# Router logits computed the other way round, and the work in front of the attention loop reordered

## What is computed

```
# block 1: attention, 16 heads of 64, one shared key/value head, a null key from cond_64
q = l2norm(ln(x) @ Wq) * q_scale;  k = l2norm(ln(x) @ Wk) * k_scale;  v = ln(x) @ Wv
x = x + ln(softmax(8 q k^T + relative bias + mask, null column) v @ Wout)
# block 2: mixture of 8 experts (the best 2) and a shared one of double width
logits = (x @ wt.T + cond_64 @ wg.T) / 2          # one of 8 per token
scores = softmax(logits); w = top 2 of scores, divided by their sum
y = sum_k w_k * (leaky(x @ w_gate[e_k]) * (x @ w_up[e_k])) @ w_down[e_k] + shared part
x = x + y
```

## Time and profile before

| | |
|---|---|
| median of 3 runs | 1135.11 us (1134.98 to 1137.51) |
| profiled execution | 1139.32 us, its span 1137.4 us |
| mean granted TensorE clock | 0.976 |
| busy, share of the span | TensorE 90%, VectorE 69%, ScalarE 46%, POOL 39% |
| chain that ended last | TensorE 66%, VectorE 20%, ScalarE 5%, issue 6% |

### The profile page before, as it was taken

How to read it: one execution, slowest core, us unless ns; L and a number is a source line. 1 busy time by engine, 2 the same in 40 slices (tenths; PEclk the granted TensorE clock), 3 DMA queues, 4 the chain that set the end, 5 groups by cost and what they waited for, 6 DMA issues and landing times.

```text
span 1137.4 us, 22612 instructions
## 1 busy us (share of the span) xinstructions
PE 1028.3 (90%) x7340; PEld 843.4 (74%) x7340; DVE 781.0 (69%) x2538; ACT 526.0 (46%) x1563; POOL 443.3 (39%) x422
## 2 busy tenths in 40 slices
PE   2377899999999999899999999899998999999898
PEld 1265587777877788677877787777877778777777
DVE  6768858775687648775587747876597756866442
ACT  2048724663356614655255623565146642566111
POOL 3154414553435505453336424354145433355112
PEclk9688999999999999999999999999999999999999
DMA  5064411321123212321123111221113211232033
GB/s 203 19 177 158 150 38 56 104 85 57 40 80 98 66 40 74 103 66 38 58 91 96 59 55 58 92 68 65 59 56 103 84 38 33 81 103 65 20 104 119
DMA packets 40939, 89.89 MB, mean 79 GB/s; under 512 B 4128, under 2 KB 18976, under 8 KB 40304
## 3 DMA queue, kind: packets, MB, share of 16 engines
q1 hardware_dynamic: 40816, 88.29, 24.3%
HBM read 78.67 MB, written 11.70 MB: 79 GB/s over the span
## 4 chain that ended last, share of the span: by engine, by line
PE 66%; DVE 20%; issue 6%; ACT 5%; POOL 1%; DMA 1%; SPq 1%; DVEq 0%; ACTq 0%; POOLq 0%
PE psY L1460 11%; PE psO L1393 6%; PE psS L1363 5%; PE psG L63 4%; PE psG L65 4%; PE psG L64 4%; PE psT L1374 3%; PE psS L63 3%; PE psS L64 3%; DVE work L1042 3%; PE psS L65 3%; PE psS L1358 2%; PE psO L1396 2%; PE psT L63 2%; PE psT L65 2%
## 5 line engine op out<-in xcount | busy, mean ns | idle before, releaser
L552 POOL TENSOR_TENSOR work<-work,rden 128x514 f32<-128x514 f32 x128 | 134.3, 1049 | 329.1 <-DVE rden L1023 328.5
L1460 PE MATMUL psY<-Wd,H 128*128 128x256 f32 x640 | 166.7, 395 | 3.7 <-POOL H L566 3.7
L675 ACT ACTIVATE work<-work,low 128x257 f32<-128x257 f32 x256 | 128.3, 503 | 80.7 <-DVE low L1042 80.6
L63 PE MATMUL psG<-x1T_hi,Wgu 128*128 128x512 f32 x280 | 128.1, 458 | 11.7 <-ACT leaky L707 9.8
L1460 PEld LDWEIGHTS psY<-Wd,H 128*128 128x128 f32 x640 | 113.3, 189 | 32.3 <-issue 15.6
L1042 DVE CUSTOM_DVE_ANT_0 work<-psS,bias,null_s 128x256 f32<-128x256 f32 x256 | 113.0, 478 | 18.3 <-PE psS L1363 18.0
L1132 DVE SCALAR_TENSOR_TENSOR leaky<-leaky 128x512 f32<-128x512 f32 x80 | 55.6, 695 | 101.5 <-ACT leaky L707 100.5
L541 POOL TENSOR_TENSOR rq<-qss,neghalf 128x16 f32<-128x16 f32 x32 | 93.7, 2930 | 55.0 <-DVE qss L1017 55.0
L65 PE MATMUL psG<-x1T_lo,Wgu 128*128 128x512 f32 x280 | 110.3, 394 | 0.0
L64 PE MATMUL psG<-x1T_hi,Wgu 128*128 128x512 f32 x280 | 109.6, 391 | 0.0
L667 ACT ACTIVATE qT_hi<-psO 128x256 fp32r<-128x256 f32 x128 | 48.9, 382 | 108.8 <-PE psO L1396 107.7
(11 more groups left out here) (242 smaller groups left out, 2677.4 us busy)
## 6 DMA issues: line engine op xcount, KB each, us to landing
Wgu<-wexp SPq DMA_DIRECT2D x80, 512.0 KB, 3.5
Wb<-wscr SPq DMA_DIRECT2D x64, 256.0 KB, 3.7
wexp<-Wgu SPq DMA_DIRECT2D x10, 512.0 KB, 2.9
xin<-in_x SPq DMA_DIRECT2D x8, 512.0 KB, 4.1
xres<-in_x SPq DMA_DIRECT2D x8, 512.0 KB, 5.0
out<-work SPq DMA_DIRECT2D x8, 512.0 KB, 3.1
H<-in_wgu SPq DMA_DIRECT2D x10, 256.0 KB, 3.8
bscr<-bscr SPq DMA_DIRECT2D x1, 2048.0 KB, 13.0
```

The source lines that it names most:

```text
L63: te.matmul(dst, a_hi, b_hi, start=start, stop=False)
L552: pool.tensor_tensor(T1[sl][:, hs, :], T1[sl][:, hs, :], rden[sl][:, 1, hs].unsqueeze(2) .to_broadcast([P, 2, N + 1]), ALU.mult)
L675: act.activation(T1[sl][:, h, :], T1[sl][:, h, :], ACT.Exp, scale=-1.0, bias=low[sl][:, 1, h:h + 1], accum_out=den[sl][:, 1, h:h + 1])
L1460: mm = te.matmul(psY[:, t // 2, (t % 2) * D:(t % 2 + 1) * D], H[:, k % H_RING, t * P:(t + 1) * P], Wd[:, ORDER[k], :], start=(k == 0 and t ...
```

## The change

The router's logits are computed with Wt as the stationary operand: WtP holds [Wt_hi, Wt_lo] (16 columns), so that two matmuls of 512 columns with x1T_hi and two with x1T_lo give 16 rows of psO, of which rows 0 to 7 and 8 to 15 have to be added. ScalarE copies them to LT; `turn_logits` multiplies LT by I2 (two identities of 8 on top of each other), which adds and transposes them into psY, from where `router_logits` reads. WT becomes the first 8 rows of LT.

ScalarE makes both halves of x1T_hi and all of KB_hi; VectorE makes KB_lo in one operation. `null_scores` uses tensor_reduce over an axis of length 1 instead of tensor_copy. The subtraction of the maximum becomes a function of its own behind `sum_q` 1. Gate 0 stands right behind the logits and no longer waits for the router; both query halves of tile 3 stand in front of gate 1, up 1 between the turned queries, gate 2 behind them. Three of the four half downs of blocks 0 and 1 move to loop steps 1 to 3. The orders of ScalarE and VectorE follow. Behind the last attention VectorE puts leak 0 and hidden 0 between the router's parts, and ScalarE the exponential and WT behind gates 0 and 1.

```diff
-DOWN_AT = {4: (2, FIRST), 5: (2, SECOND), ...
+DOWN_AT = {1: (0, SECOND), 2: (1, FIRST), 3: (1, SECOND), 4: (2, FIRST), 5: (2, SECOND), ...
@@ scalar: attention
-                    if t >= 2 and moe is not None:
-                        take_gate(moe, t - 2)
+                    if t == 2 and moe is not None:
+                        take_gate(moe, 0)
+                        softmax(moe)
...
                     if t == 1:
                         if moe is not None:
-                            softmax(moe)
+                            logits(moe)
                         need(act, kdT_ps, r, 1)
-                        act.activation(KB[0][0:DH, :, :], psO[0:DH, :]...
+                        act.activation(KB[0][:, :, :], psO[:, :]...
+                if moe is not None:
+                    take_gate(moe, 1)
                 for n in range(4):
                     turned_q(r, n)
-                    if n == 1 and moe is not None:
-                        take_gate(moe, 2)
+                if moe is not None:
+                    take_gate(moe, 2)
...
             def route(m):
-                need(act, x1T_ps, m, 1)
-                act.activation(x1T[0][:, 0, :], psG[:], ACT.Copy).then_inc(x1T_a.sem, 1)
+                for c, bank in ((0, psG), (1, psO)):
+                    need(act, x1T_ps, m, c + 1)
+                    act.activation(x1T[0][:, c, :], bank[:], ACT.Copy).then_inc(x1T_a.sem, 1)
+
+            def logits(m):
+                need(act, lt_ps, m, 1)
+                need(act, wscr_in, m - 1, 16)
+                act.activation(LT, psO[0:2 * E, :], ACT.Copy).then_inc(lt_done.sem, 1)
@@ vector: attention
                 sum_q(r, 1)
+                if moe is not None:
+                    router_shift(moe)
                 need(dve, kdT_ps, r, 1)
-                dve.tensor_copy(KB[0][DH:P, :, :], kT[DH:P]).then_inc(kb_v.sem, 1)
-                for i, ev in ((0, kb_a), (1, kb_v)):
...
+                need(dve, kb_a, r, 1)
+                dve.tensor_tensor(KB[1][:, :, :], psO[:, :]..., KB[0][:, :, :]..., ALU.subtract)
...
                 sum_q(r, 2)
                 if moe is not None:
                     router_best(moe)
+                scale_q(dve, r, 1, qn_done)
+                sum_q(r, 3)
+                if moe is not None:
                     leak(moe, 1)
-                scale_q(dve, r, 1, qn_done)
-                if moe is not None:
-                    hidden(moe, 1)
-                sum_q(r, 3)
                 for n in range(4):
                     turned_q(r, n)
                     if n == 1 and moe is not None:
-                        leak(moe, 2)
+                        hidden(moe, 1)
                         router_weights(moe)
+                scale_q(dve, r, 2, qn_done)
                 if moe is not None:
+                    leak(moe, 2)
                     hidden(moe, 2)
-                scale_q(dve, r, 2, qn_done)
                 scale_q(dve, r, 3, qn_done)
@@ tensor: attention
                     logits(moe)
+                    gate(moe, 0)
+                    turn_logits(moe)
                 need(te, kd_done, r, 1)
...
-                if moe is not None:
-                    gate(moe, 0)
                 q_half(2, 1).then_inc(q_ps.sem, 1)
                 if moe is not None:
                     up(moe, 0)
                 need(te, qs_done, r, 2)
                 q_half(3, 0)
+                q_half(3, 1).then_inc(q_ps.sem, 1)
...
                 if moe is not None:
                     gate(moe, 1)
-                q_half(3, 1).then_inc(q_ps.sem, 1)
-                if moe is not None:
-                    up(moe, 1)
                 for n in range(4):
                     turn_q(r, n)
                     if n == 1 and moe is not None:
-                        gate(moe, 2)
+                        up(moe, 1)
                 if moe is not None:
+                    gate(moe, 2)
+                    down(moe, 0, FIRST)
                     up(moe, 2)
-                    down(moe, 0, WHOLE)
-                    down(moe, 1, WHOLE)
...
             def logits(m):
+                need(te, x1T_v, m, KC)
+                for c in range(KC):
+                    te.matmul(psO[0:2 * E, :], WtP[:, c, :], x1T[0][:, c, :], start=(c == 0), stop=False, ...)
+                for c in range(KC):
+                    mm = te.matmul(psO[0:E, :], WtP[:, c, 0:E], x1T[1][:, c, :], start=False, stop=(c == KC - 1), ...)
+                mm.then_inc(lt_ps.sem, 1)
+
+            def turn_logits(m):
+                need(te, lt_done, m, 1)
+                need(te, ysum, m - 1, TILES)
                 for t in range(TILES):
+                    mm = te.matmul(psY[:, 0, t * E:(t + 1) * E], LT[:, t * P:(t + 1) * P], I2, start=(t == 0), stop=True, ...)
                 mm.then_inc(lg_ps.sem, 1)
```

More of the change, by code:

```diff
@@ L136, in attention_moe @@
         PARTS = ("hi", "lo")
-        Wall = [sb(f"Wall_{part}", [P, KC, E + KVN + HEADS * DH], F32R) for part in PARTS]
-        KV0, Q0 = E, E + KVN
+        Wall = [sb(f"Wall_{part}", [P, KC, KVN + HEADS * DH], F32R) for part in PARTS]
+        KV0, Q0 = 0, KVN
+        WtP = sb("WtP", [P, KC, 2 * E], F32R)
+        I2 = sb("I2", [2 * E, E])[:]
         Wout = [sb(f"Wout_{part}", [P, PAIRS, D], F32R) for part in PARTS]
@@ L715, in _ @@
             route(ROUNDS - 1)
-            softmax(ROUNDS - 1)
-            weights(ROUNDS - 1)
+            logits(ROUNDS - 1)
             for k in range(BLOCKS):
                 take_gate(ROUNDS - 1, k, True)
+                if k == 0:
+                    softmax(ROUNDS - 1)
+                if k == 1:
+                    weights(ROUNDS - 1)
         @block.vector
@@ L801, in kv_parts @@
             def kv_parts():
[L802 to L805, removed]
+                for src, hi, lo in ((Wkvn_in, *(part[:, :, KV0:Q0] for part in Wall)),
+                                    (Wt[:], WtP[:, :, 0:E], WtP[:, :, E:2 * E])):
+                    pre(dve.tensor_copy(hi, src))
+                    pre(dve.tensor_tensor(lo, src, hi.bitcast(F32), ALU.subtract))
             def others():
@@ L1030, in null_scores @@
                 for tile, T, n in ((1, T1, N), (0, T0, P)):
[L1031 to L1032 removed]
+                    dve.tensor_reduce(T[sl][:, :, n], null_s[:, 2 * bb + tile, h0:h0 + GH].unsqueeze(2), AX, ALU.add)
             def scores(r, g, s):
@@ L1119, in x1_parts @@
             def x1_parts(m):
[L1122 to L1125, removed]
+                for c, bank in ((0, psG), (1, psO)):
+                    need(dve, x1T_a, m, c + 1)
                     dve.tensor_tensor(x1T[1][:, c, :], bank[:], x1T[0][:, c, :].bitcast(F32),
@@ L1158, in _ @@
             router_logits(m)
+            router_shift(m)
+            leak(m, 0)
             router_best(m)
+            hidden(m, 0, True)
             router_weights(m)
-            for k in range(BLOCKS):
+            for k in range(1, BLOCKS):
                 leak(m, k)
@@ L1408, in logits @@
             def logits(m):
[L1409 removed]
+                need(te, x1T_v, m, KC)
+                for c in range(KC):
+                    te.matmul(psO[0:2 * E, :], WtP[:, c, :], x1T[0][:, c, :], start=(c == 0), stop=False, skip_group_check=True)
+                for c in range(KC):
+                    mm = te.matmul(psO[0:E, :], WtP[:, c, 0:E], x1T[1][:, c, :], start=False, stop=(c == KC - 1),
+                                   skip_group_check=True)
+                mm.then_inc(lt_ps.sem, 1)
+            def turn_logits(m):
+                need(te, lt_done, m, 1)
+                need(te, ysum, m - 1, TILES)
                 for t in range(TILES):
[L1411 to L1415 removed]
+                    mm = te.matmul(psY[:, 0, t * E:(t + 1) * E], LT[:, t * P:(t + 1) * P], I2, start=(t == 0), stop=True,
+                                   skip_group_check=True)
                 mm.then_inc(lg_ps.sem, 1)
@@ L1484, in _ @@
                 gate(m, k, True)
+                if k == 0:
+                    turn_logits(m)
                 up(m, k, True)
```

50 lines of the change are left out of this document (21 added, 29 removed).

## The result

The changed kernel takes 1119.2 us (median of 4 runs, 1117.63 to 1119.3) against 1135.05 us before: ratio 0.9855, 95% interval 0.9837 to 0.9872. The forecast was 1124.1, so the gain is 15.9 us where 11.0 was predicted. The profiled execution took 1119.15 (span 1117.4).

The account below looks back on a forecast made before the run. TensorE, 90% busy, bounds the kernel, VectorE second in front of the loop. Work 1.04 less and waits 3.15 against 3.49 give 1.4 us a round, 9.8 in seven; plus 1.1 and 0.1, 11.0: 1124.1 us, range 1114 to 1133.

Parts of the forecast that it names:

- The rounds: Whole loop: seven equal rounds of 130.5 us, one of them walked; 129.1 us a round after the change.
- Work: TensorE at the router logits: 2.88 us removed, 0.92 for logits and 0.92 for turn_logits added; 1.04 us saved a round.
- LT: In front of turn_logits: TensorE waits 0.55 us for ScalarE's copy LT, which ends at 433.6.
- Front's waits: TensorE up to step 5: waits 0.55, 0.35, 0.85, 1.0 and 0.4, in all 3.15 us against 3.49 before.
- Null reductions: Step 4 on VectorE: reductions avoid the copies' wait, removing score 5's 0.44 us a round; bounds 0 to 0.75.
- Last expert part: Behind the last attention: lg as before but gate 0 done, gate 2 at 1092.5 instead of 1093.62; 1.1 us.
- A: Work alone: waits keep their 3.49 us, 8 us gained, 1127; chance 0.70 together with the forecast.
- B: Front of the loop: a third or so of the 3.15 us waits left, 3 us a round, 1113; chance 0.12.
- C: VectorE parked behind lg: slower if lg comes after 436.2; at 437.0 0.8 us a round, 1140; chance 0.08.
- D: Steps 5 to 20: savings taken back by VectorE or ScalarE waits, within 3 us of 1135; chance 0.10.

Follow-up runs that it names:

- idle matmuls: Changed kernel plus four unused 128x512 matmuls a round, ahead of the logits in one kernel, between scores 0 and 1 in another: 1126.55 and 1120.12 us.
- gate 0 moved: Changed kernel with gate 0 put behind turn_logits and the keys' transposes (kd): 1131.15 us, ratio 0.9958.
- null copies: Changed kernel with the null scores' tensor_reduce turned back into tensor_copy: 1123.2 us, ratio 0.9901.
- downs in the waits: Changed kernel with down 0's halves before and behind gate 2, and down 1's halves at loop steps 0 and 1: 1118.13 us, ratio 0.9846.
- VectorE's load put back: Changed kernel with one x1T_hi half and the half-height key operations back on VectorE: 1132.06 us, ratio 0.9965.
- the shift moved: Kernel before with the router's maximum subtraction (lgc) moved behind sum 1 and ScalarE's exponential behind take_gate 0: 1136.1 us, ratio 0.9997.
- downs in front: Changed kernel with the downs of blocks 0 and 1 whole in front of the loop, behind up 2: 1129.18 us, ratio 0.9942.

## Why the prediction was right, and where its sizes were off

- *The rounds.* The prediction took them as seven equal ones. They are not: before, the fourth to the sixth are longer in front of the loop, and the last is 127.2 us. The round it walked is of the usual kind up to score 5.
- *Work.* Logits 0.93 (0.92 predicted), turn_logits 0.99 (0.92, where 8 x 0.11 is 0.88): 0.96 us less a round instead of 1.04. The idle matmuls show that added work at this place counts in full in the changed kernel.
- *LT.* The step that failed: I had a wait of 0.55 at turn_logits; the trace has none in six of the seven rounds and 0.2 in one. The durations of the walk were right, its anchor was not. VectorE's first operation of the round starts 1.39 us after the x1 transposes (422.64), where I kept the 1.96 of before; with it sum 0, Square 1 (4.94 instead of 5.4) and LT come half a us earlier, and LT ends at 428.59, 0.2 before TensorE is free for it. VectorE is not quicker there: in both rounds it starts 2.53 us after its last work on x. It is TensorE that starts the transposes later, by 0.56 us of "issue", where the one round that I walked had none; over the second to the sixth round of before the anchor is 1.46 to 1.96, and 1.39 to 1.81 after. That LT holds nothing up hangs on gate 0 as cover, as the kernel with gate 0 moved shows.
- *Front's waits.* Take gate 1 0.27 (0.35), hidden 1 0.83 (0.85), score 1 1.23 (1.0), score 2 0.49 (0.4). Up 3 and up 4 wait no more, nor does the first weighed down. Sum of the waits up to step 5: 2.82 against 3.15 predicted; with work 0.96 less, 3.49-2.82+0.96 = 1.63 a round, and 1.70 was measured at score 5. That is the term that was mis-sized, by LT's wait of 0.55, of which score 1's longer wait took some back: 0.3 a round, 2 us in all.
- *Null reductions.* Taken as 0.44 a round up to score 5; bringing the copies back shows 0.27 there in six rounds and nothing in the seventh. The 4.0 us of the medians are more than this, and where the rest of them lies is not shown.
- *Last expert part.* 2.2 instead of 1.1. lg comes 7.7 us after the x1 transposes there, before 8.35, and TensorE waits 1.19 for the turned weights:

```profile
1066.96 1.05 PE L1436 MATMUL psY<-I,LT 16*128 16x8 f32 x8
...
1073.53 0.60 PE L1443 MATMUL psO<-ident,oh 128*8 128x128 f32 x4 [1.19 <-DVE oh L1132]
1073.88 0.47 PE L63 MATMUL psT<-x1T_hi,Wgu 128*128 128x512 f32 x1
```

  Gate 2 follows 13.6 us after the x1 transposes, where it took 15.5 before. Some 0.7 of the 2.2 are the clock's: over the first 8.35 us of this part the granted clock was 0.59 before and 0.80 after. Three experiments with the changed kernel's last part had 0.59 there too (null copies, gate 0 behind, downs in the waits), and their last part took 57.8 us, against 57.1 in the changed kernel and 59.3 before: 1.5 at a like clock. The walk also priced turn_logits at 0.9 in a stretch that it took at half clock, where its own row has 0.22 a record, 1.8.
- *Rivals.* A (work alone, 1127) is near what the kernels with the downs or VectorE's load put back show, 1129 and 1132: both parts are needed to go beyond it. The single parts' costs (12.9, 10.0, 12 and 4.0 us) add up to far more than the gain, since each leans on the others. B had the right suspicion on the LT wait, but 2.8 of its 3.15 us of waits do come. C did not occur: lg stands at 8.76, well before its deciding point of 10.5. Its mechanism is real: with the idle matmuls ahead of the logits lg stands at 9.67, 0.9 later, and so does score 5. D is excluded: no lead at score 5 changes by more than 0.1 up to the round's last turn.
- *What stays open.* The rounds' 11.4 and the last part's 1.5 at a like clock make 12.9 of the medians' 15.9. In the profiled pair the clock adds 1.5 in the last output projection and 0.7 behind it; whether the medians have that too is not shown, though the other kept trace with the old front (the shift moved) has 0.59 in that projection as well, and of the ten with the new one only the one with gate 0 moved has. Another 1.7 stand ahead of the first x1 transposes: they start at 163.34 instead of 164.99, but at 161.9 to 163.1 in the five experiments on the changed kernel that leave that stretch as it is (downs in front, gate 0 moved, downs in the waits, both with idle matmuls), so that it moves by 1.4 us by itself. How often lgc collides with POOL in other executions of before is not known either.

## What to carry to other kernels

Ask of each saved or added microsecond where it lies: it counts in full ahead of a point for which the follower already waits, and for next to nothing in front of a wait that another engine ends. Make the follower thinner first, then move filler work into the waits that its chain leaves; each wait filled exposes the next engine's, here POOL's, which has then to be started earlier as well. Put a block of independent work between an operation and the copy that it needs from another engine. Don't take one round's distance between two engines' starts for all rounds: read it in each.

## What the runs showed of the hardware that I had not expected

- A VectorE subtraction of 128x32 elements with both inputs in SBUF takes 0.19 us, and up to 1.89 when POOL's 1.91 us multiply is under way: it ends with that multiply, so not its own size sets the loss but what is left of the other's instruction. The Trainium skill (SBUF — State Buffer, Who interferes with whom) has a VectorE instruction with two inputs in SBUF contend with a GpSimd instruction that reads SBUF, and issue order decide who blocks; the traces agree (POOL at 696.80, lgc at 696.86). The changed kernel keeps one such collision, in front of which TensorE does not wait: at step 4 the same kind of addition lasts 1.20 beside POOL's 1.28 us multiply at 462.20, where at step 0 it takes 0.19.

```profile
462.33 1.20 DVE L1027 TENSOR_TENSOR null_s<-null_s,null_bias 128x32 f32<-128x32 f32 x1
```

- Where gate 0 was moved, two rounds out of seven had a stretch at a lower granted clock behind a wait for LT of 1.33 and 1.72 us, and a third, with 1.30, had none. The two profiled executions of before and after also differ in the clock of the last output projection, 0.59 and 1.00 over its first 4.2 us, without an edit there and with the same wait of 0.93 us in front of it.
